# A 3x3 box filter finished by three accumulating transfers to the output

## The reference

```python
x = x + _L0_conv_ref(_gn(x), ...)   # 1x1 convolution with weights mixed per image (sparsemax gate over 8 experts)
x = x + _L1_conv_ref(_gn(x), ...)   # 3x3 depthwise, BN, relu, prune; 1x1 convolution, BN, relu, prune
x = x + _L2_conv_ref(_gn(x), ...)   # attention with squared, normalised queries and keys
x = x + _L3_conv_ref(_gn(x), 0)     # 3x3 box filter per channel, zero padding
return x
```

```python
kernel = jnp.full((C, 1, 3, 3), 1.0 / 9.0, dtype=x.dtype)
out = jax.lax.conv_general_dilated(x, kernel, window_strides=(1, 1), padding=((1, 1), (1, 1)),
                                   feature_group_count=C, ...)
```

## Time and profile before

| | |
|---|---|
| median of three runs | 1625.53 us (1621.58 to 1627.81) |
| the profiled execution, its own time | 1624.92 us |
| its span, first to last instruction | 1623.1 us |
| mean granted TensorE clock in it | 0.973 |
| busy: TensorE / VectorE / ScalarE / GpSimd | 1530.0 / 1376.0 / 1362.3 / 189.1 us |
| mean busy share of the 16 DMA engines, queue of SP | 9.6% |
| bytes moved | 55.58 MB |

### The profile page before, as it was taken

One profiled execution on the slowest core, in us unless ns is written; L12 is line 12 of the kernel. 1 busy time (PEld: TensorE's weight loads), 2 busy tenths in 40 slices (PEclk: granted clock), 3 DMA queues, 4 the chain that ended last, 5 costly groups with the idle time before them and its releaser, 6 DMA issues. The chain is left out here.

```text
span 1623.1 us, 26428 instructions
## 1 busy us (share of the span) xinstructions
PE 1530.0 (94%) x8190; PEld 1149.4 (71%) x8190; DVE 1376.0 (85%) x2466; ACT 1362.3 (84%) x3496; POOL 189.1 (12%) x142
## 2 busy tenths in 40 slices
PE   4469999999999999999999999999999999999993
PEld 2247777777777777777777777777777777776773
DVE  5877689999888998988889998888999988888446
ACT  3368998988999888899998889999888899987862
POOL 1111011011110101111011111101101111010000
PEclk8689999999999999999999999999999999999996
DMA  4000011000111110011111001111100011000001
GB/s 148 20 20 21 21 40 41 31 29 22 40 40 40 40 40 20 20 40 40 40 40 40 20 20 40 40 40 40 40 27 28 24 40 40 21 21 21 21 20 40
DMA packets 21058, 55.58 MB, mean 34 GB/s; under 512 B 2321, under 2 KB 3345, under 8 KB 21010
## 3 DMA queue, kind: packets, MB, share of 16 engines
q1 hardware_dynamic: 20914, 54.98, 9.6%
q10 hardware_dynamic: 96, 0.00, 0.0%
HBM read 29.29 MB, written 25.69 MB: 34 GB/s over the span
## 5 line engine op out<-in xcount | busy, mean ns | idle before, releaser
L770 DVE SCALAR_TENSOR_TENSOR h<-xpad,dw_sb,h 128x784 f32<-128x784 f32 x512 | 495.9, 1031 | 0.0
L541 PE MATMUL tile_ps<-wqk,xn_parts 128*112 128x512 f32 x1344 | 363.8, 425 | 0.0
L541 PEld LDWEIGHTS tile_ps<-wqk,xn_parts 128*112 128x112 f32 x1344 | 235.3, 175 | 79.6
L583 PE MATMUL tile_ps<-k,xT 112*128 112x256 f32 x896 | 205.2, 388 | 7.7 <-ACT xT L1026 7.7
L583 PEld LDWEIGHTS tile_ps<-k,xT 112*128 112x128 f32 x896 | 174.3, 195 | 40.2 <-issue 8.4
L449 PE MATMUL conv_ps<-h,pw_masked 128*128 128x392 f32 x512 | 180.5, 496 | 5.5 <-issue 5.5
L960 ACT ACTIVATE junk<-x 128x784 bf16<-128x784 f32 x192 | 162.3, 848 | 23.6 <-DVE x L797 15.5
L571 PE MATMUL conv_ps<-x,mixed 128*128 128x392 f32 (+1 forms) x512 | 175.1, 494 | 2.2 <-ACT mixed L994 1.1
L1234 POOL TENSOR_SCALAR pw_masked<-pw_sb,hmask 128x256 f32<-128x256 f32 x64 | 119.1, 1869 | 433.9 <-DVE hmask L778 425.5
L1221 POOL TENSOR_SCALAR xpad<-x,gn_r,gn_s 128x784 f32<-128x784 f32 x64 | 64.4, 1013 | 894.2 <-DVE gn_s L701 894.2
L449 PE MATMUL conv_ps<-xn_parts,w_out 128*128 128x392 f32 x768 | 152.7, 347 | 0.0
(11 more groups left out here) (138 smaller groups left out, 2646.9 us busy)
## 6 DMA issues: line engine op xcount, KB each, us to landing
x<-x SPq DMA_DIRECT2D x32, 784.0 KB, 4.3
out<-x SPq DMA_DIRECT2D x32, 784.0 KB, 3.4
expert_sb<-expert_rows SPq DMA_DIRECT2D x8, 256.0 KB, 5.2
x<-w_qk SPq DMA_DIRECT2D x1, 512.0 KB
x<-w_vT SPq DMA_DIRECT2D x1, 256.0 KB
x<-w_ln SPq DMA_DIRECT2D x1, 256.0 KB
pw_sb<-pw_wT SPq DMA_DIRECT2D x1, 256.0 KB
gmean<-group_mean SPq DMA_DIRECT2D x1, 64.0 KB, 3.8
```

The source lines that it names most:

```text
L541: mm = nc.tensor.matmul(bank, xn2_parts[:, u, i, m * TOK:(m + 1) * TOK], wqk[:, v, i, :], start=False, stop=(i == J - 1 and u == 1))
L583: mm = nc.tensor.matmul(tile_ps[:, KX_BANK, i * C:(i + 1) * C], xT[:, m, half(i)], k2[:, m, :], start=(m == 0), stop=(m == M - 1))
L770: ins = nc.vector.scalar_tensor_tensor(acc, view, scalar, acc, ALU.mult, ALU.add)
```

## The change

x3 is stored as soon as make_x3 has written it. The factor 1/9 is moved into the normalisation: a new small VectorE instruction, `box_scale`, multiplies the scale and shift of the fourth layer by 1/9, and ScalarE applies these. VectorE makes only the first two box passes, the row sums. The vertical sum is made by three transfers that GpSimd issues, each adding one of three row-shifted views of row_sums (784 KB each) to the image in the output tensor in HBM. They are issued one after another: each waits for the one before it, the first for the row sums and for the store of x3. VectorE waits, before it writes row_sums for the next image, for all three transfers of the image before.

```diff
@@ sp, step @@
-                if F.active:
-                    sp.wait_ge(x4_ready.sem, x4_ready.at(F))
-                    sp.dma_start(out_dram[F.times(1)], x3[:, F.odd]).then_inc(stored.of(F), 16)
+                if E.active:
+                    sp.wait_ge(x3_ready.sem, x3_ready.at(E))
+                    hold(sp, "sp")
+                    sp.dma_start(out_dram[E.times(1)], x3[:, E.odd]).then_inc(stored.of(E), 16)
@@ vector @@
+            def box_scale(A, F):
+                dve.wait_ge(gn.sem, gn.at(A))
+                if (F - 1).active:
+                    dve.wait_ge(x3pad_ready.sem, x3pad_ready.at(F - 1))
+                nc.vector.tensor_scalar(box_rs[:], gn_rs[:, :, 3, :], 1.0 / TAPS, None, ALU.mult).then_inc(box_scaled.sem, 1)
...
             def make_x3(E):
                 if (E - 2).active:
                     dve.wait_ge(stored.of(E - 2), stored.at(E - 2))
+                    dve.wait_ge(x3pad_ready.sem, x3pad_ready.at(E - 2))
...
-            def box_sums(F, steps):
...
-            def make_x4(F):
...
+            def box_row_sums(F):
+                dve.wait_ge(x3pad_ready.sem, x3pad_ready.at(F))
+                dve.wait_ge(setup_pool, SETUP_POOL)
+                if (F - 1).active:
+                    for rows in rows_added:
+                        dve.wait_ge(rows.of(F - 1), rows.at(F - 1))
+                nc.vector.tensor_tensor(*row_operands(0), ALU.add).then_inc(row_step.sem, 1)
+                dve.wait_ge(row_step.sem, row_step.at(F, 1))
+                nc.vector.tensor_tensor(*row_operands(1), ALU.add).then_inc(row_step.sem, 1)
@@ vector, step: box_scale(A, F) behind scales_shifts(A), box_row_sums(F) in the place of box_sums @@
@@ scalar @@
-            def normalise_x3(A, F):
+            def normalise_x3(F):
                 if (F - 1).active:
-                    act.wait_ge(x4_ready.sem, x4_ready.at(F - 1))
-                normalise(A, 3, ...)
+                    act.wait_ge(row_step.sem, row_step.at(F - 1))
+                act.wait_ge(box_scaled.sem, box_scaled.at(F))
+                for j in range(J):
+                    nc.scalar.activation(x3pad[:, j, 1:1 + H, 1:1 + W], x3[:, F.odd, j, :].rearrange("p (h w) -> p h w", w=W),
+                                         ACT.Identity, bias=box_rs[:, 1, j:j + 1],
+                                         scale=box_rs[:, 0, j:j + 1]).then_inc(x3pad_ready.sem, 1)
@@ gpsimd, step: add_rows(F) behind mask_weights(C_) @@
+            def add_rows(F):
+                pool.wait_ge(row_step.sem, row_step.at(F))
+                pool.wait_ge(stored.of(F), stored.at(F))
+                for n in range(BOX_ROWS):
+                    if n:
+                        pool.wait_ge(rows_added[n - 1].of(F), rows_added[n - 1].at(F))
+                    hold(pool, "pool")
+                    rows = row_sums[:, :, n:n + H, :].rearrange("p j h w -> p j (h w)")
+                    pool.dma_start(out_dram[F.times(1)], rows, accum_op=ALU.add).then_inc(rows_added[n].of(F), 16)
```

More of the change, by code:

```diff
@@ L25 @@
 M = HW // TOK
-BOX_STEPS = 4
+BOX_ROWS = 3
 STRIPS = 4
@@ L185, in build @@
         gn_sd = sb("gn_sd", [P, 4, J])
-        gn_r = sb("gn_r", [P, 4, J])
-        gn_s = sb("gn_s", [P, 4, J])
+        gn_rs = sb("gn_rs", [P, 2, 4, J])
+        gn_r, gn_s = gn_rs[:, 0], gn_rs[:, 1]
+        box_rs = sb("box_rs", [P, 2, J])
         pooled = sb("pooled", [P, 2, J])
@@ L235, in build @@
         stored = DmaCount([sem("stored_even"), sem("stored_odd")])
+        rows_added = [DmaCount([sem(f"rows{n}_added_even"), sem(f"rows{n}_added_odd")]) for n in range(BOX_ROWS)]
         gn = sig("gn", GN_DONE)
@@ L310, in box_operands @@
             return [(sums, x3pad[:, :, 1:1 + H, 0:W], inner),
-                    (sums, sums, x3pad[:, :, 1:1 + H, 2:2 + W]),
-                    (inner, row_sums[:, :, 0:H, :], sums),
-                    (inner, inner, row_sums[:, :, 2:2 + H, :])][n]
+                    (sums, sums, x3pad[:, :, 1:1 + H, 2:2 + W])][n]
         def conv_banks(j):
@@ L383, in _ @@
                 sp.wait_ge(stored.of(last), stored.at(last))
+                for rows in rows_added:
+                    sp.wait_ge(rows.of(last), rows.at(last))
         @block.tensor
@@ L698, in scales_shifts @@
                 dve.wait_ge(gn_sqrt.sem, gn_sqrt.at(A))
-                nc.vector.reciprocal(gn_r[:], gn_sd[:]).then_inc(gn.sem, 1)
+                nc.vector.reciprocal(gn_r, gn_sd[:]).then_inc(gn.sem, 1)
                 dve.wait_ge(gn.sem, gn.at(A, GN_R))
-                nc.vector.scalar_tensor_tensor(gn_s[:], gn_avg[:, :, 0:2], -1.0, gn_r[:], ALU.mult,
+                nc.vector.scalar_tensor_tensor(gn_s, gn_avg[:, :, 0:2], -1.0, gn_r, ALU.mult,
                                                ALU.mult).then_inc(gn.sem, 1)
+            def box_scale(A, F):
[3 more added lines that the diff above has]
+                nc.vector.tensor_scalar(box_rs[:], gn_rs[:, :, 3, :], 1.0 / TAPS, None, ALU.mult).then_inc(box_scaled.sem, 1)
             def gate_logits(A):
@@ L886, in step @@
                     scales_shifts(A)
+                if F.active:
+                    box_scale(A, F)
                 if E.active:
@@ L1154, in step @@
                 if F.active:
-                    normalise_x3(A, F)
+                    normalise_x3(F)
                 if C_.active:
@@ L1242, in step @@
                     mask_weights(C_)
+                if F.active:
+                    add_rows(F)
             run(pool, step)
```

14 lines of the change are left out of this document (5 added, 9 removed).

## The result

The changed kernel takes 1644.51 us, the median of four runs (1643.37 to 1644.92), against 1626.18 us of the kernel before (four runs, 1621.58 to 1627.81). The ratio is 1.0116, with a 95% interval of 1.0098 to 1.0135: 1.2% slower. The forecast was 1652, range 1630 to 1684, slower.

What follows compares the result with a forecast made beforehand. TensorE was taken to bound the steady step, hiding the adds; the end pays six links. The time is 1603.1 + 6D, 1651.1 for D = 8, with VectorE's relief of 4 included; 0.6 to the median gives 1652, range 1630 to 1684.

Steps and rivals of the forecast that it cites:

- adds hidden: Steady state: all 96 adding transfers but the last six covered, with room for links of up to 14 us.
- part 1: VectorE's queue: two make_x4 passes and box steps 2 and 3 go, box_scale comes; -4 us for the run.
- D: Time of one chain link, from GpSimd seeing a semaphore to the next rising: 8.0 us, bounds 3.7 to 11.4.
- The steady gain: Steady steps: reciprocals 3.7 us sooner, shortening TensorE's wait for kx_low; 3.5 us for the run, bounds 0 to 4.3.
- The drain: Step at 1455: ScalarE's 1.1 us wait of xT copies, behind VectorE's late reciprocal, half regained; bounds 0 to 1.1.
- Part 2: x3 stored right after make_x3, ahead of the box sums: costs nothing, since the next load goes out at the same moment.
- R2: Rival: not slower, adds go nearly at a store's price, links below 5.1 us; chance 0.10, of which 0.02 faster.
- R3: Rival: link dearer than its three legs end to end, 11.4 to 14 us, still hidden in steady state; 1672 to 1687; chance 0.08.
- R4: Rival: steady state breaks with links beyond 14 us, GpSimd late with xpad; 1834 us at 16 us links; chance 0.08.
- The descriptor mechanism: GpSimd cannot write descriptors while VectorE holds the shared port pair in a two-port mode; matters only if it doubled link time.

Runs made afterwards that it cites:

- load_box: Changed kernel plus two idle VectorE passes of 128x1568 where box steps 2 and 3 stood, ahead of the reciprocals: 1661.45 us, ratio 1.0228 to the kernel before.
- load_x4: Changed kernel plus two idle VectorE passes of 128x784 where make_x4 stood, behind the reciprocals: 1646.06 us, ratio 1.0128 to the kernel before.
- passes_moved: Kernel before, without adding transfers, with box steps 2 and 3 moved behind the reciprocals: 1615.07 us, ratio 0.9937 to the kernel before.
- load_both: Changed kernel plus idle VectorE passes both where box steps 2 and 3 and where make_x4 stood: 1661.88 us, ratio 1.0229 to the kernel before.
- halves: Changed kernel with each adding transfer cut into two channel halves of 392 KB, two independent chains of three: 1641.83 us, ratio 1.0094 to the kernel before.
- two_buffers: Changed kernel with two row_sums buffers, VectorE waiting for the adds of two images before: 1638.59 us, ratio 1.0083 to the kernel before.
- late_store: Changed kernel with the store of x3 moved back behind the row sums of the same image: 1651.23 us, ratio 1.0152 to the kernel before.
- no_adds: Changed kernel without its 96 adding transfers and the waits for them, output lacking the box filter: 1601.82 us, ratio 0.9853 to the kernel before.
- plain_writes: Changed kernel with the three transfers overwriting instead of adding, output only one row of the box sum: 1624.83 us, one run.
- one_add: Changed kernel with one adding transfer per image instead of three, output lacking two of three rows: 1614.07 us, one run.
- tail2_dve: Changed kernel with images 30 and 31 finished by VectorE box steps 2 and 3, x4 and a plain store: 1615.34 us, ratio 0.9938 to the kernel before.
- load_box_scale_late: load_box with box_scale behind kx_low instead of ahead of it: 1662.78 us, ratio 1.0232 to the kernel before.

## Why the prediction was right, and where it was off

**The direction and the reason.** Steady state TensorE's, adds hidden, and an end that pays two chains of three links with the row sums between them: all of it as predicted, and the step of 46.70 just below the 46.8 to 47.0 that was to be seen. The sum from the end of image 30's row sums was 52.0 forecast, 51.3 measured. That it is so near is in part luck: the links were 0.36 us shorter each, 2.2 in all, and what comes after the last landing 1.6 longer. The 7.5 us between the forecast 1652 and 1644.5 are nearly all in part 1.

**The link.** D was put at 8.0: a load and a store end to end, 7.7, and a hop of 0.3. It is 7.64: 7.1 to landing and 0.53 from the landed data to the next issue. That a load and a store make a good sum is an analogy that came out; no run shows the legs of an adding transfer apart. The estimate of D = 6.0 that the prediction worked out from the Trainium skill (Collectives: The Full Stack, "The bandwidth ceiling") was too low. The page's ratio of two holds roughly: 7.1 against 3.9 for the plain write is 1.8. What the last link pays on top was underestimated: from its issue to the end are 9.06 us, 2.0 more than the landing, where 0.4 had been taken over from the kernel before. The sum had no term for GpSimd's closing DRAIN.

**Part 1, the term that was mis-sized.** VectorE's relief was put at -4; the end of image 30's row sums came 10.9 us sooner, 6.7 of it in the steady steps and 4.2 in the drain. Both lie outside the bounds that the prediction gave, 0 to 4.3 and 0 to 1.1:

- The steady gain was taken as 0.14 us per step (3.5 over the run) from the idle time that the weight loads of kx_low's product show, and is 0.30. The place was right: in the mean over 20 steps this product starts 0.14 us earlier after the previous block in the changed kernel, and everything behind it 0.23, and a further 0.07 is gained at the products that wait for xT. The step that failed is the cap: the gain was limited to what the rows show as TensorE's wait for kx_low, 0.18 us per step, but TensorE gained 0.23 there, and 0.07 more at a place where the earlier trace rows list no wait of TensorE. The cause given, the reciprocals, is shown by load_box against load_x4 and by passes_moved.
- The drain was put at -0.5 and gave -4.2. The wait that was named there did shrink by about what was taken, from 3.5 to 2.8 us for TensorE (L583, L586 in the changed kernel); the rest was not foreseen. The windows of its three steps, before and after:

```profile
1455.40:1499.70 44.30, 40.33 (x215) 31.66 (x214) 37.43 (x57) 36.77 (x95) 5.70 (x4) 0.96 0.05 19
1499.70:1543.70 44.00, 41.06 (x221) 32.67 (x220) 21.22 (x38) 36.61 (x95) 3.75 (x2) 0.96 0.05 19
1543.70:1584.80 41.10, 37.68 (x205) 30.72 (x204) 18.66 (x34) 27.35 (x79) 0.00 (x0) 0.92 0.05 20
```

```profile
1448.40:1493.50 45.10, 42.18 (x218) 33.44 (x217) 32.06 (x54) 36.72 (x95) 9.30 (x7) 0.92 0.37 72
1493.50:1536.70 43.20, 40.26 (x226) 32.41 (x225) 15.90 (x35) 36.41 (x95) 7.47 (x5) 1.00 0.39 75
1536.70:1573.90 37.20, 33.77 (x200) 27.75 (x199) 13.24 (x31) 27.30 (x79) 3.58 (x3) 1.00 0.42 82
```

The column ahead of the DMA share is the granted clock. Shares not granted: 44.3 x 0.04 + 44.0 x 0.04 + 41.1 x 0.08 = 6.8 us before, 45.1 x 0.08 = 3.6 after, with shares rounded to 0.01. The lower of TensorE's two levels (1.2 instead of 2.4 GHz) is half, so the time at it is twice that; summed over finer windows it is 13.7 us before and 6.8 after. The first of these stretches began at 1489.5, behind this wait (start us, us):

```profile
1488.40 5.81 PE L583 MATMUL tile_ps<-k,xT 112*128 112x256 f32 x18 [3.47 <-ACT xT L1026]
```

What this is worth is read off kernels with the same work of TensorE in the drain but another share of clock. From the 31st start of gn_s to the last but one, in the one profiled execution of each:

| kernel | us | of them at 1.2 GHz |
|---|---|---|
| before | 223.0 | 13.7 |
| load_both | 223.3 | 13.7 |
| halves | 221.4 | 13.7 |
| two_buffers, load_x4 | 220.1, 220.2 | 10.2 |
| after, passes_moved | 218.8, 218.9 | 6.8 |

Halves has VectorE's light queue and the long stretches: 2.6 us over the changed kernel. Two_buffers, with the middle ones, lies half way. So 2.6 of the 4.2 us are clock, and 1.6 (223.0 - 221.4) are left for VectorE's queue, and here too for its order: passes_moved, with all of VectorE's work and the short stretches, is as fast as the changed kernel. The same 2.6 are in the gain of passes_moved, and the middle stretches make most of the 1.5 us by which load_x4 is slower than the changed kernel. Why one execution gets the long ones and another the short ones was not settled.

**Part 2, the store.** "Cost nothing" holds, but late_store shows that the old place would have cost 6.7 us here. The sum had this in it without a term of its own, since it let the adds begin at the end of the row sums.

**The rivals.** R2 needed D below 5.1; that is what a plain write issued by GpSimd has (4.4), and no adding one. R3 and R4 needed D above 11.4. GpSimd's slow mask instructions, which spoke for R4, are as slow without any adds (1.87 us each in no_adds), and GpSimd's issue took the same 1.2 us beside VectorE's depthwise passes (768.14) as alone at the end (1632.64). The descriptor mechanism that the Trainium skill describes (SBUF — State Buffer, "SBUF: two separate sides") did not show here; the page ties it to VectorE's two-port modes, and no run shows whether any of these passes is in one, so the mechanism as such was not tested.

## What to carry to other kernels

Work taken off an engine that does not set the pace is worth what stands behind it in its queue: here the order of two passes against a few small instructions that another engine waited for was worth all of the steady gain, and it cost no new transfer. Do not cap such a gain by the wait rows: they showed 0.18 us per step of the 0.30. A chain of dependent transfers that is free in every step is paid in full at the end, twice over if one buffer ties two images together; price the end on its own, with what the issuing engine still does after its last issue, and finish the last images another way. An adding transfer took 1.8 times as long as a plain one to land.

## What the runs showed of the hardware

- GpSimd's issue of a transfer of 784 KB took 1.20 us for an adding and 0.72 us for a plain one, and 0.86 for an adding half: it shrinks less than the bytes.
- When transfers issued by GpSimd came last, the span ended with GpSimd's closing DRAIN, 2.0 us after the last landing in the changed kernel, plain_writes, late_store and two_buffers, 1.6 in one_add (one transfer per image) and 4.0 in halves (six). Where SP's store came last (the kernel before, passes_moved, tail2_dve) it was 0.4.
- With three adds per image the median time to landing of the loads rose from 4.3 to 5.6 us in the changed kernel and 7.3 in late_store, but only to 4.4 in load_box; with one add per image it was 4.3. That seems to go by how far the third add is when the load is issued: in a steady step 5.4 us after the add's issue in the changed kernel, 1.6 in late_store, 5.8 in load_box. The step was 46.70 us with loads of 4.3, 5.6 and 7.3 us alike.
- A VectorE instruction on 128 x 2 elements takes 0.2 us by itself and up to 0.95 when it starts while GpSimd works on xpad (in the changed kernel `pooled`, 0.77 in the mean over 30 such cases). Which instruction is hit moves with the queue; in load_box_scale_late it was box_scale, at a mean of 487 ns instead of 170.
